# Two transformer layers on one core: row order of the query and key stacks, and the place of the first layer's query loads

## The reference

```
x = x + layernorm(attn_L0(layernorm(x)))     # low-rank q and kv, rotary part, 16 heads of 16
x = x + layernorm(ffn_L0(layernorm(x)))      # silu(gate) * up, int8 weights with scales
x = x + layernorm(attn_L1(layernorm(x)))     # plain q, k, v with biases, 16 heads of 16
x = x + layernorm(ffn_L1(layernorm(x)))
# attn: probs = softmax(causal(q @ k.T) * scale); y = probs @ v; y @ W_o.T + b_o
```

## Time and profile before

| what | us |
|---|---|
| median of 3 runs | 1207.25 (1206.73 to 1210.45) |
| the profiled execution, whole | 1213.39 |
| its span in the profile | 1211.1 |
| outside the span | 2.3 |
| PE busy | 1129.4 (93% of the span) |
| VectorE (DVE) busy | 1004.0 (83%) |
| ScalarE (ACT) busy | 794.6 (66%) |
| GpSimd (POOL) busy | 349.6 (29%) |

### The profile page before, as it was taken

How to read it: one execution, slowest core, us unless ns; L and a number is a source line. 1 busy time by engine, 2 the same in 40 slices (tenths; PEclk the granted TensorE clock), 3 DMA queues, 4 the chain that set the end, 5 groups by cost and what they waited for, 6 DMA issues and landing times.

```text
span 1211.1 us, 37127 instructions
## 1 busy us (share of the span) xinstructions
PE 1129.4 (93%) x15000; PEld 574.3 (47%) x15000; DVE 1004.0 (83%) x2648; ACT 794.6 (66%) x1606; POOL 349.6 (29%) x598
## 2 busy tenths in 40 slices
PE   6689999999999999899998989999999999998996
PEld 4434434444444443655664334444444445465664
DVE  6569989999899774777878999999999888548786
ACT  4445868878888998344452456878888888944332
POOL 4424210122211224434343321113121112424443
PEclk8789999999999999999998999999999999999999
DMA  5333231212100000010220340041120000000001
GB/s 164 92 91 109 64 103 43 49 29 49 35 2 3 3 4 3 1 36 16 63 79 29 110 119 25 15 102 35 29 55 3 3 3 3 4 2 1 19 18 35
DMA packets 31818, 49.92 MB, mean 41 GB/s; under 512 B 7266, under 2 KB 24436, under 8 KB 31639
## 3 DMA queue, kind: packets, MB, share of 16 engines
q1 hardware_dynamic: 25664, 42.30, 12.9%
q0 software_dynamic: 5408, 4.87, 1.6%
q10 hardware_dynamic: 576, 0.39, 0.1%
HBM read 32.44 MB, written 14.68 MB: 39 GB/s over the span
## 4 chain that ended last, share of the span: by engine, by line
PE 70%; DVE 15%; issue 4%; ACT 3%; DMA 3%; POOL 2%; SPq 1%; POOLq 0%; ACTq 0%; DVEq 0%
PE ps L1113 67%; DVE m_tile L980 4%; DMA k_stack<-k_parts 2%; DVE ps L982 2%; ACT region_p L783 2%; PE ps L1281 1%; PE ps L1108 1%; DVE stats L855 1%; DVE k_stack L1066 1%; DVE region_p L1034 1%; DVE k_stack L1063 1%; DVE region_p L892 1%; DVE region_p L868 1%; POOL y_chunk L665 1%; DVE region_p L1054 1%
## 5 line engine op out<-in xcount | busy, mean ns | idle before, releaser
L783 ACT ACTIVATE region_p<-ps 128x512 f32<-128x512 f32 (+3 forms) x1280 | 591.3, 539 | 142.5 <-PE ps L1113 138.1
L980 DVE TENSOR_REDUCE m_tile<-ps 128x1 f32<-128x512 f32 x768 | 497.2, 684 | 31.9 <-PE ps L1113 30.1
L1113 PE MATMUL ps<-q_stack,k_stack 99*32 99x512 bf16 (+3 forms) x5120 | 401.3, 349 | 14.8 <-ACT region_p L783 7.9
L1113 PE MATMUL ps<-k_stack,q_stack 96*32 96x512 bf16 (+3 forms) x5120 | 396.1, 351 | 18.9 <-DMA k_stack<-k_parts 9.7
L1113 PE MATMUL ps<-region_p,v_all 128*17 128x512 f32 (+3 forms) x2560 | 290.1, 528 | 2.9 <-POOL region_p L653 2.8
L982 DVE CUSTOM_DVE_ANT_0 ps<-ps,causal 128x128 f32<-128x128 f32 (+3 forms) x512 | 247.6, 498 | 42.1 <-PE ps L1113 40.5
L1113 PEld LDWEIGHTS ps<-q_stack,k_stack 99*32 99x32 bf16 x5120 | 139.1, 95 | 205.7 <-ACT region_p L783 118.3
L1113 PEld LDWEIGHTS ps<-k_stack,q_stack 96*32 96x32 bf16 x5120 | 138.3, 96 | 200.5 <-DVE m_tile L980 55.5
L653 POOL TENSOR_SCALAR_AFFINE_SELECT region_p<-region_p 128x512 f32<-128x512 f32 x128 | 81.3, 637 | 266.3 <-ACT region_p L783 260.1
L1113 PE MATMUL ps<-region_a,w_ffn 128*128 128x512 f16 x512 | 121.9, 382 | 7.1 <-DVE region_a L900 6.1
L819 ACT ACTIVATE k_stack<-ps,cols 128x512 f32<-128x512 f32 x64 | 44.0, 688 | 109.2 <-PE ps L1113 106.6
(11 more groups left out here) (147 smaller groups left out, 897.1 us busy)
## 6 DMA issues: line engine op xcount, KB each, us to landing
k_parts<-parts SPq DMA_DIRECT2D x16, 384.0 KB, 2.5
q_parts<-parts SPq DMA_DIRECT2D x16, 384.0 KB, 2.6
q_stack<-q_parts SPq DMA_DIRECT2D x32, 192.0 KB
k_stack<-k_parts SPq DMA_DIRECT2D x32, 192.0 KB, 4.8
q_stack<-q_parts SPq DMA_DIRECT2D x32, 128.0 KB
k_stack<-k_parts SPq DMA_DIRECT2D x32, 128.0 KB, 5.0
X<-in_x SPq DMA_DIRECT2D x4, 512.0 KB, 7.3
q_stack<-q_parts SPq DMA_DIRECT2D x32, 64.0 KB
```

What stands on the lines that cost most here:

```text
L783: nc.scalar.activation(probs[:, o.j % SLOTS, o.h, o.off:CH], psT[:, o.k % TBANKS, o.off:CH], ACT.Exp, scale=SCALE).then_inc(s.exp_done, 1)
L980: nc.vector.tensor_reduce(maximum, scores, AX.X, ALU.max).then_inc(s.ring_free, 1)
L1113: return pe.matmul(o, a, b, start=first, stop=last)
```

## The change

Both stacks get their rows in another order inside each run: before, row = copy x 16 + component; now, row = component x n + copy. The destination rows of a DMA are the same in number and place, and the same 4 KB pieces of DRAM are read; the order in which the source is walked differs. Both stacks change alike, so that the contraction pairs the same parts. Rows 96 to 98 don't change.

In layer 0 the query loads of group 0 are issued after a wait for the store of unit u - 1 alone (the chunk's `q` unit); the wait for all stores stands behind them, ahead of the key loads. Layer 1 keeps its order.

```diff
                 def load_queries(g, c):
...
-                                     src.rearrange("s d h t -> s d (h t)").broadcast_to([n, DH, HG * CH])
+                                     src.rearrange("s d h t -> d s (h t)").broadcast_to([DH, n, HG * CH])
                                      ).then_inc(q_in[g % 2][c], 16)
                 def load_keys(g, c):
...
-                                     src.rearrange("s d h t -> s d (h t)")).then_inc(k_in[g % 2][c], 16)
+                                     src.rearrange("s d h t -> d s (h t)")).then_inc(k_in[g % 2][c], 16)
...
                     c = chunk_ready(L, u)
                     if c is not None:
-                        parts_complete(chunk_units(L, c))
-                        load_stacks(0, c)
+                        if L == 0:
+                            sp.wait_ge(parts_stored[(u - 1) % PB], stored(L, (u - 1) % PB, (u - 1) // PB + 1))
+                            load_queries(0, c)
+                            parts_complete(chunk_units(L, c))
+                            load_keys(0, c)
+                        else:
+                            parts_complete(chunk_units(L, c))
+                            load_stacks(0, c)
```

## The result

The changed kernel takes 1193.39 us (median of four runs, 1192.64 to 1194.81), the kernel before 1207.67 us beside it. The ratio of the runs on record is 0.9869, 95% interval 0.9853 to 0.9886, the quotient of the two medians 0.9882: faster by 1.2 to 1.3%. The forecast was 1193.4. The two profiles differ by more than the medians: the span goes from 1211.1 us to 1190.3.

The account below looks back on a forecast made before the run. PE's own matmuls were 67% of the chain, with 9.7 us of PE waits for stacks; gains of 6.0 + 3.0 + 1.7 + 3.1 = 13.8 us took the median 1207.25 to 1193.4, range 1187 to 1201.

Parts of the forecast that it names:

- item 1: Stack loads: rows by component spread every load over 16 engines; a pair of 0.79 MB takes 4.5 us at 177 GB/s.
- Item 2: Layer 0 query loads issued ahead of the wait for all stores: 1.1 us at chunk 0, 1.2 us at chunk 1.
- third rival: Stack copies still sit on few engines, or engines take turns; only early query loads act: 2.3 us, 1205.4, chance 0.05.
- Item 3: Key loads' issue gets dearer by the extra dimension: 0.5 us charged per key stack, on the path only at chunk 0.
- Stop 1: PE's wait for the first stack pair, chunk 0: falls from 7.5 to 1.4 us, 6.0 gained, bounds 4.2 and 7.5.
- The estimate from the 435 GB/s: First stack pair limited by its issue, landing about 39.3 us, so PE's wait there gives 6.9 us.
- Clock behind stop 1: PE's granted clock stays up after the first stack wait, from the first score unit: 3.0 us gained, bounds 0 and 3.7.
- Stop 2: PE's wait at the second stack pair, 69.45 to 71.19 us, vanishes: 1.7 us gained.
- The later loads: Group-1 loads and later waits of 1.98, 0.97 and 2.49 us shrink as m_rows lands sooner: 3.1 us, bounds 0 and 7.
- third stop: PE's 0.5 us wait for a stack at 161.7 us: goes entirely.
- the prediction's own sign of being wrong: Among the signs named as wrong: m_rows landing longer than before at 164 or 790 us.
- The slower rival: m_rows queues behind query loads on all 16 engines, landing at up to 11.7 us: time 1219, chance 0.03.

Follow-up runs that it names:

- experiment 3: The early query loads alone, rows in the old order, against the kernel before: 1209.45 us, ratio 0.9976.
- experiment 2: The new row order alone, queries again waiting for all stores, against the kernel before: 1200.12 us, ratio 0.9894.
- experiment 4: The changed kernel again, no edit, on the chip of the two halves, against the kernel before: median 1198.19 us, ratio 0.988.
- experiment 8: The kernel before plus 28 filling matmuls on constants ahead of the first score unit, against the kernel before: 1208.6 us, ratio 0.998.
- experiment 1: The kernel before, unchanged, profiled and timed once more: ratio 0.9998.
- Experiment 9: The changed kernel plus a wait holding group 2's query loads until step 4's m_rows land, in both layers, against the kernel before: 1193.54 us, ratio 0.9846.
- experiment 5: The changed kernel with the new row order for layer 0's group-0 stacks alone, against the kernel before: ratio 0.9899.
- experiment 6: The changed kernel with the new row order in layer 0 alone, against the kernel before: ratio 0.9896.

## Why the prediction was right, and where its parts were not

**Why the load was slow, item 1.** Right, and shown: 96 small packets, no tail (result); 69 and the tail with the old order (experiment 3); the row order alone does 0.0106 of the 0.012 (experiment 2). That the tail ran on few engines is also in the earlier trace rows: from 43 to 46 us the DMA share is 0.10, 1.6 of 16 engines. The tail was read too evenly, since its slices go from 14 to 82 GB/s.

**Item 2, the early loads.** 1.1 us of SP's time at chunk 0 were expected. Experiments 2 and 4 differ by 1.0 us from the mark to the first score unit (5.3 and 4.3). By itself the part gives 2.9 us, a little over the 2.3 of the third rival (its 0.5 us for the keys' issue falls away with the old order).

**Item 3, dearer key issue.** Right in size: 1.80 us for a key stack, not 1.34.

**Stop 1.** 2.04 us were left, not 1.4; the mark to the score unit shrank by 5.4 us, not 6.0. The data passed in 4.0 us where the full engines' rate had given 4.5; from the end of the last key issue (35.90) to the first score unit it took 2.6 us, where 2.2 was taken. The estimate from the 435 GB/s of the Trainium skill's page "DMA: Bandwidth & Descriptors", section "Specifications", had left 0.5 us of the stop; 2.04 were left, so the measurement decides against it.

**Clock behind stop 1.** 3.0 us were expected. The two profiles give 3.6, near the bound of 3.7; by experiment 8, whose clock fell later on, it is 2.1 to 3.1. Taking it as a yes or no was wrong. In the seven profiles that are the changed kernel's up to 57 us, leaving out the filled one, the clock stayed up behind stop 1 six times and fell once; behind both profiles of the kernel before it fell, as it did behind the 6.0 us of experiment 3 and the 2.87 of experiment 2.

**Stop 2.** The term was mis-sized: 1.7 us were expected, and step 0 to step 1 shrank by 3.6. I had looked at the stop alone; between the kernel before and a profile without a fall the clock adds 1.9 in the first pair. The stop was the smaller part of it: in experiment 1 it was 0.47 us and the stretch still 3.1 longer than without a fall, in experiment 8 there was no stop and it was 3.8 longer. In three of those seven profiles the clock fell there, and the stretch took 28.6 to 30.5 us.

**The later loads, 3.1 us.** Here the step failed by its mechanism, at 170.6 us: I took the stop to go with the query backlog, and it stayed (1.98 and 1.86). The backlog only moved from few engines to all: m_rows landed after 3.6 to 4.4 us, where I had counted on 2.4. That was the median of the four loads, but PE waits for the slowest, and this one went only from 4.6 to 4.4. By the median (2.4 to 3.8) the prediction's own sign of being wrong, m_rows landing later than before at 164 us, came true. The slower rival had named this, with too high a price: 4.4 us, not 11.7. Experiment 9 takes the loads away from it and the stop ends. The clock behind that stop, which stands in the prediction only as a bound (about 1 us), gave 1.5 in the first pair. The two stretches of layer 1 shrank by 0.8 and 2.5 us in the first pair, and were 0.8 to 1.3 and 0.9 to 1.7 longer in experiments 5 and 6 than with the new order there. The 0.5 us at the third stop went, but it is also gone in experiments 3 and 5, which have the old order for group 1. (Half of the 5.4 us is 2.7, not 2.6.)

**The sum.** 13.8 expected, 14.3 measured, and 14.7 and 14.9 on the other chips. It came out this near since the errors cancel: 0.6 too much at stop 1, too little at stop 2, and a mix of executions with and without a fall for the clock. That the forecast of 1193.4 met the median to the tenth is luck. The profiles' 20.8 us is not the change's size: 2.4 us lie ahead of the change, and the profile before had every fall, the profile after none.

## What to carry to other kernels

Count the packets of a load that lands late: rows plus completion packets tell on how many engines it runs, and a broadcast or another short dimension that stands outermost keeps it on few, with everything issued behind it. Before a transfer is made faster, ask which small load that an engine waits for is issued in its midst, and hold back what isn't needed yet; that was a further stop of 0.6 to 2.1 us here. And take several profiles before a difference between two is given to a change: here one program's own executions differ by up to 9 us (experiment 4), and in the profiles a fall of the clock in the first 80 us costs 2.5 to 4.7 us each time.

## What had not been expected of the hardware

- The granted clock fell in one execution and not in another of the same program with the same gaps: behind a stop of 1.63 us it fell to 0.55, behind 2.04 and 1.83 us it stayed at 1.00. In all three profiles with filling ahead of the first score unit it fell some 8 us behind it, in one of them (0.83 and 0.74) where PE was busy for 7.6 of 8 us; in the six of the same stretch with neither filling nor a fall behind stop 1 it stayed up. The runs don't settle what decides it; that PE's longer gaps make it likelier is what the profiles agree with (7.3 to 7.5, 6.0 and 2.9 us: four falls in four).
- 16 engines that are full with 4 KB rows move less than few would suggest. In the tail a DMA share of 0.10, 1.6 engines, went with 41 GB/s, some 26 for each busy engine; at 94.7% of 16 engines it was 177, some 12 for each. No run here shows why.
- The extra dimension of the source costs 0.46 us of issue for a key stack, 1.80 against 1.34; the query stacks, which had it before, stay at 1.88 against 1.98.
